# Router logits of the adaLN/FFN kernel: four column groups by tokens instead of by channels, turned by VectorE

## The reference, cut to what matters

```python
y = einsum('boi,bih->boh', agg_w, x) + agg_b[:, :, None]      # _L0_cond_ref, per sample
router_logits = y.reshape(-1, 1024) @ gate_w.T                # gate_w is 8 x 1024
routing = softmax(router_logits, axis=1)                      # 8 experts
in_scale, out_scale = routing @ in_channel_scale, routing @ out_channel_scale
out = y * in_scale @ sign(weight).T * out_scale + bias
x = x + out
```

## Time and profile before

| | us |
|---|---|
| median of 3 runs | 541.09 (540.41 to 542.42) |
| the profiled execution, own time | 541.51 |
| its span in the trace | 539.7 |
| TensorE busy (matmul records) | 523.5 |
| VectorE busy | 301.5 |
| ScalarE busy | 121.6 |
| GpSimd busy | 253.3 |

### The profile page before, as it was taken

One profiled execution on the slowest core, in us unless ns is written; L12 is line 12 of the kernel. 1 busy time (PEld: TensorE's weight loads), 2 busy tenths in 40 slices (PEclk: granted clock), 3 DMA queues, 4 the chain that ended last, 5 costly groups with the idle time before them and its releaser, 6 DMA issues.

```text
span 539.7 us, 14212 instructions
## 1 busy us (share of the span) xinstructions
PE 523.5 (97%) x5717; PEld 446.1 (83%) x5717; DVE 301.5 (56%) x482; ACT 121.6 (23%) x291; POOL 253.3 (47%) x121
## 2 busy tenths in 40 slices
PE   5897999999999999999999999999999999999997
PEld 4675778788787898898988988989889889898895
DVE  4579998797775654447446354364453634734411
ACT  5733334444434330101101011010010110101100
POOL 0028766766767398154263360651623616426100
PEclk9999999999999999999999999999999999999999
DMA  8696455554667362532413414224143162251111
GB/s 304 230 403 226 164 194 175 204 204 167 194 221 231 110 211 84 123 108 56 147 66 110 128 47 145 98 63 149 52 120 118 42 159 85 76 145 55 40 40 39
DMA packets 55049, 74.68 MB, mean 138 GB/s; under 512 B 6192, under 2 KB 41200, under 8 KB 55024
## 3 DMA queue, kind: packets, MB, share of 16 engines
q1 hardware_dynamic: 54800, 73.96, 42.4%
q10 hardware_dynamic: 224, 0.36, 0.3%
HBM read 57.50 MB, written 16.79 MB: 138 GB/s over the span
## 4 chain that ended last, share of the span: by engine, by line
PE 92%; DVE 4%; ACT 2%; issue 1%; DMA 1%; SPq 0%; DVEq 0%; ACTq 0%
PE bank L639 54%; PE bank L525 19%; PE bank L620 5%; PE bank L682 4%; PE bank L451 3%; PE bank L464 2%; PE bank L498 2%; DVE parts L978 1%; PE bank L601 1%; DVE y_t L949 1%; DMA cst<-in_consts 1%; ACT late L754 1%; PE bank L474 0%; PE bank L481 0%; DVE y_t L971 0%
## 5 line engine op out<-in xcount | busy, mean ns | idle before, releaser
L639 PE MATMUL bank<-early,parts 128*128 128x320 f32 (+1 forms) x1152 | 206.7, 337 | 0.0
L639 PEld LDWEIGHTS bank<-early,parts 128*128 128x128 f32 x1152 | 184.6, 188 | 16.6
L525 PE MATMUL bank<-late,parts 128*128 128x512 f32 x512 | 129.5, 403 | 2.1 <-DVE work L986 2.1
L525 PEld LDWEIGHTS bank<-late,parts 128*128 128x128 f32 x512 | 93.3, 190 | 23.0 <-DVE work L986 2.9
L1222 POOL TENSOR_TENSOR xs<-raw 128x1024 f32<-128x1024 f32 x14 | 26.5, 1894 | 157.1 <-DMA raw_turned<-x_scratch 157.1
L978 DVE TENSOR_TENSOR parts<-y_t,parts 128x512 fp32r<-128x512 f32 x64 | 95.0, 1503 | 2.5 <-ACT parts L785 1.0
L639 PE MATMUL bank<-late,parts 128*128 128x512 f32 x384 | 94.1, 394 | 0.0
L639 PEld LDWEIGHTS bank<-late,parts 128*128 128x128 f32 x384 | 70.9, 188 | 15.9
L1170 POOL TENSOR_TENSOR work<-work 128x512 f32<-128x512 f32 x32 | 46.3, 1448 | 47.3 <-DVE work L986 46.1
L1114 DVE TENSOR_TENSOR qk<-bank,qk 128x256 f32<-128x256 f32 x16 | 6.8, 424 | 102.1 <-ACT qk L874 102.1
L785 ACT ACTIVATE parts<-y_t 128x512 fp32r<-128x512 f32 x62 | 38.5, 631 | 88.3 <-DVE y_t L1093 46.1
(11 more groups left out here) (111 smaller groups left out, 484.7 us busy)
## 6 DMA issues: line engine op xcount, KB each, us to landing
xs<-in_x SPq DMA_DIRECT2D x16, 512.0 KB, 3.3
work<-in_x SPq DMA_DIRECT2D x16, 512.0 KB, 3.3
x_scratch<-work SPq DMA_DIRECT2D x16, 512.0 KB, 3.0
raw<-x_scratch SPq DMA_DIRECT2D x128, 64.0 KB, 2.9
work<-x_scratch SPq DMA_DIRECT2D x16, 512.0 KB, 3.6
out_tokens<-work SPq DMA_DIRECT2D x15, 512.0 KB, 2.7
raw_turned<-x_scratch SPq DMA_DIRECT2D x112, 64.0 KB, 2.5
stage<-in_wearly SPq DMA_DIRECT2D x8, 576.0 KB, 4.0
```

The lines of the kernel that those rows point to most:

```text
L525: last = mm(bank[4 + h][:, :], parts[:, p, a, c, :], signs[:, c, h * HALF:(h + 1) * HALF], start=(k % 16 == 0), stop=(k % 16 == 15))
L639: return mm(dst, parts[:, p, a, c, :], w(b, c), start=(k == 0), stop=(close and k == 23))
```

## The change

`product_logits` now gives column group t the tokens 32t to 32t+31 instead of a quarter of the channels. For each chunk c and each group t it multiplies the gate's 128x32 block with y_t's 128 channels x 32 tokens into partitions 32t to 32t+31, columns 0 to 31 of bank 2; all 8 chunks add up in each group. So 32 products with 32 moving columns take the place of 8 with 128, and each group holds a finished 32 (experts, padded) x 32 (tokens) block. VectorE transposes the four blocks in one instruction into SBUF (`turn_logits`), which gives 128 tokens x 32 with the 8 logits first. `copy_logits` on ScalarE and `sum_logits` on TensorE go, as do the selection matrix (8 columns of the constants) and their semaphores. `route_max` and `gate_exps` read SBUF. `product_scales` waits for `logits_turned` in place of `logits_copied`, `product_logits` for an earlier half of `scale_in` (two tiles back) in place of `gate_exp`, and `turn_logits` for `gate_exp` of the tile before.

```diff
             def product_logits(i, p, first_tile=False):
                 pe.wait_ge(y_biased, 4 * i + 2 * p + 2)
                 if not first_tile:
-                    pe.wait_ge(gate_exp, 2 * i + p)
+                    pe.wait_ge(u_ready, 4 * i + 2 * p - 3)
                 for c in range(L8):
-                    at = slice(EP * (c % 4), EP * (c % 4) + EP)
-                    made = mm(bank[2][at, 0:P], cst[:, C_GATE + c * EP:C_GATE + (c + 1) * EP], y_t[:, p, c, :],
-                              start=(c < 4), stop=(c >= 4))
+                    for t in range(P // EP):
+                        tokens = slice(EP * t, EP * t + EP)
+                        made = mm(bank[2][tokens, 0:EP], cst[:, C_GATE + c * EP:C_GATE + (c + 1) * EP], y_t[:, p, c, tokens],
+                                  start=(c == 0), stop=(c == L8 - 1))
                 made.then_inc(logits_made, 1)
-
-            def sum_logits(i, p, first_tile=False):
-                pe.wait_ge(logits_copied, 2 * i + p + 1)
-                if not first_tile:
-                    pe.wait_ge(u_ready, 4 * i + 2 * p - 1)
-                mm(bank[2][:, 0:E], logits_t[:, :], cst[:, C_SEL:C_SEL + E], start=True, stop=True).then_inc(logits_done, 1)
...
-            def product_scales(i, p, first_tile=False, copied=1):
+            def product_scales(i, p, first_tile=False, turned=1):
                 pe.wait_ge(routing_split, 2 * i + p + 1)
-                pe.wait_ge(logits_copied, 2 * i + p + copied)
+                pe.wait_ge(logits_turned, 2 * i + p + turned)
...
-                    if k == SUM_AT and two:
-                        sum_logits(*two)
...
-            def copy_logits(i, p):
-                act.wait_ge(logits_made, 2 * i + p + 1)
-                do(logits_t[:, :], bank[2][:, 0:P], ACT.Copy).then_inc(logits_copied, 1)
-
             def gate_exps(i, p):
                 act.wait_ge(gate_max, 2 * i + p + 1)
-                do(gate[:, 8:16], bank[2][:, 0:E], ACT.Exp, bias=gate[:, 0:1], accum_out=gate[:, 1:2]).then_inc(gate_exp, 1)
+                do(gate[:, 8:16], logits[:, 0:E], ACT.Exp, bias=gate[:, 0:1], accum_out=gate[:, 1:2]).then_inc(gate_exp, 1)
...
+            def turn_logits(i, p, first_tile=False):
+                dve.wait_ge(logits_made, 2 * i + p + 1)
+                if not first_tile:
+                    dve.wait_ge(gate_exp, 2 * i + p)
+                v.transpose(logits[:, :], bank[2][:, 0:EP]).then_inc(logits_turned, 1)
+
             def route_max(i, p):
-                dve.wait_ge(logits_done, 2 * i + p + 1)
-                v.tensor_reduce(gate[:, 0:1], bank[2][:, 0:E], AX.X, ALU.max, negate=True).then_inc(gate_max, 1)
+                dve.wait_ge(logits_turned, 2 * i + p + 1)
+                v.tensor_reduce(gate[:, 0:1], logits[:, 0:E], AX.X, ALU.max, negate=True).then_inc(gate_max, 1)
...
                 if four:
                     mix_kernels(*four)
+                if two:
+                    turn_logits(*two)
                 scale_out(i, p, 0)
                 scale_in(*one)
```

More of the change, by code:

```diff
@@ L52 @@
 C_W1, C_W2, C_CW = 162, 290, 298
-C_GATE, C_ID, C_SEL = 362, 618, 746
-C_RLO, C_SLO, C_SSG = 754, 755, 756
-C_END = 757
+C_GATE, C_ID = 362, 618
+C_RLO, C_SLO, C_SSG = 746, 747, 748
+C_END = 749
 PRODUCTS = ((0, 0), (0, 1), (1, 0))
-TURN_AT, BLOCK_AT, SUM_AT, CONV0_AT = 7, 18, 26, 4
+TURN_AT, BLOCK_AT, CONV0_AT = 7, 18, 4
 LORA_AT = 11
@@ L105, in adaln_ffn_kernel @@
         gate = sb("gate", [P, 64])
-        logits_t = sb("logits_t", [P, P])
+        logits = sb("logits", [P, EP])
         qk = sb("qk", [P, 2, NQK // 2])
@@ L173, in adaln_ffn_kernel @@
         logits_made = sem("logits_made")
-        logits_copied = sem("logits_copied")
-        logits_done = sem("logits_done")
+        logits_turned = sem("logits_turned")
         gate_max = sem("gate_max")
@@ L534, in _ @@
             product_logits(0, 0, True)
-            sum_logits(0, 0, True)
             inputs_of_y(0, 1)
@@ L554, in period0 @@
                             product_y(*three)
-                        product_scales(*one, copied=2 if two else 1)
-                    if k == SUM_AT and two:
-                        sum_logits(*two)
+                        product_scales(*one, turned=2 if two else 1)
                     ffn0_step(i, p, k)
@@ L563, in _ @@
                     pe.wait_ge(u_ready, 1)
-                    product_logits(0, 1)
+                    product_logits(0, 1, True)
                 if k == 10:
                     inputs_of_y(1, 0)
-                    sum_logits(0, 1)
                     product_y(1, 0)
@@ L574, in _ @@
                     product_y(1, 1)
-                    product_scales(0, 1, copied=2)
-                if k == 28:
-                    sum_logits(1, 0)
+                    product_scales(0, 1, turned=2)
                 ffn0_step(0, 0, k, True)
@@ L805, in round_u @@
                 round_parts(i, p, y_t[:, p], u_ready, u_hi, by_block)
-            copy_logits(0, 0)
             gate_exps(0, 0)
@@ L822, in _ @@
             copy_out_scale(0, 0, 1, False)
-            copy_logits(0, 1)
             gate_exps(0, 1)
@@ L827, in _ @@
             round_routing(0, 1)
-            copy_logits(1, 0)
             round_u(0, 1, True)
@@ L841, in period0 @@
                     round_stage(0, NW, (chunk + 1) * 16, early[:, 0, bass.ds(chunk, 1), :].rearrange("p a n -> p (a n)"))
-                if two:
-                    copy_logits(*two)
                 if one:
@@ L997, in _ @@
                                    ALU.mult, ALU.add).then_inc(scale_ready, 1)
+            turn_logits(0, 0, True)
             route_max(0, 0)
@@ L1010, in _ @@
             mix_kernels(1, 0)
+            turn_logits(0, 1)
             route_max(0, 1)
@@ L1015, in _ @@
             split_routing(0, 1)
+            turn_logits(1, 0)
             scale_out(0, 0, 0)
@@ L1262, in lay_out @@
     consts[:, C_GATE:C_ID].reshape(P, L8, EP)[:, :, 0:E] = turned(f["L0_ffn_gate_w"])
-    consts[:, C_SEL:C_SEL + E] = np.arange(P)[:, None] % EP == np.arange(E)[None]
     consts[:, C_ID:C_ID + P] = np.eye(P, dtype=np.float32)
```

## The result

The changed kernel takes 546.66 us in the median of 4 runs (546.31 to 547.10), the kernel before 541.75 beside it: ratio **1.0094**, 95% interval 1.0072 to 1.0116. It is slower by 5 us (0.9%); 540.0 was forecast, and 546.7 lies above the range. The price came from neither of the places where the prediction looked for one.

A forecast was written before the change was run, and what follows sets the result against it. TensorE, busy 97% of the span, was taken to bound the kernel. Sum -2.2 us and logits +1.1 us gave -1.1 us: 541.51 to 540.4, and 540.0 us with the median 0.4 us lower; range 538.8 to 544.4 us.

The forecast's parts named there:

- The sum goes: TensorE, dense stretch: dropping `sum_logits` from between the large products saves 0.22 us a tile, -2.2 us for ten tiles.
- The logits become 32 narrow products: TensorE's logits block, dense stretch: 0.68 us against 0.57, +0.11 us a tile, +1.1 us for ten.
- The straight line: Length of a logits round: 0.78 ns a column and 7 ns fixed, from 128 and 64 columns; 0.032 us at 32.
- Copy, transpose and the wait: ScalarE loses 16 copies, VectorE gains 16 transposes of 0.2 us; in the dense stretch nothing is lost.
- The start: Before 75 us: the third tile's logits still wait for a load of x until about 30.0 us; nothing gained.
- rival 1: Logits block: rounds do not shrink below 64 columns, block 1.10 us, kernel 544.2 us; 26 in 100.
- its own point of decision (0.79): From a logits block of 0.79 us on, a round of 0.039 us, the kernel is slower than before.
- Rivals 2 and 3: Logits records one after another, 551 us, 3 in 100; VectorE's transpose late, five periods wait, 542.0 us, 6 in 100.
- The 0.5 us at 43 us and its return: The scales' wait at 43.61 us shrinks by 0.5 us; TensorE's wait in the next block, near 56 us, gives it back.
- The range: Kernel time from 538.8 to 544.4 us, given 79 in 100.

The follow-up runs named there:

- experiment 5: The changed kernel with the logits of only the first 16 tokens of each group of 32, so 16 moving columns for 32; 546.19 us in one run.
- Experiments 1 and 2: Tiny unread products added: at 6 us to the changed kernel (544.27 to 541.63 us) and kernel before (541.91); ahead of kernel before's first four logits (546.12).

## Why the prediction was wrong

- **The sum goes, -0.22 us a tile: right.** 21 large products follow the scales in 99.12 - 94.19 = 4.93 us; in TensorE's timeline of before, the same 21 with the sum among them took 92.89 - 87.75 = 5.14. That is 0.21.
- **The logits become 32 narrow products, +0.11 us a tile: right in size, in part by luck,** 0.69 against 0.57, +0.12. The straight line was carried beyond its last point, and experiment 5 shows that it would have been wrong one step further: at 16 columns it gives 0.2 us less for the rounds, and 0.03 was measured. What sets a round at 32 columns is the floor of 0.033 us, and the line's 0.032 happens to lie on it. The rule of the Trainium skill ("TensorEngine Tiling (Array Packing)", Instruction Overhead: about 60 cycles a matmul) asked for y's 1.10 us here and is not what happens: 32 columns take 0.69. Its advice against tiling an already small dimension is right for the step to 16.
- **Copy, transpose and the wait: right.** 0.20 to 0.22 us for 0.2, no gap in the dense stretch. The period fell by 0.07 to 0.095 us where -0.11 was forecast; the ten tiles gave 0.9 us for 1.1.
- **The start: the step that failed.** "Late next is this load: nothing gained" and the words before it took the first 30 us as waits of the program alone and costed the edit's 96 more instructions a tile at nothing. The third tile's logits came 4.8 us late (34.8 us, forecast 30.0), the seventh's 6.4 us. Experiments 1 and 2 show that it is the number of instructions: with the block ends shifted, 2.4 to 5.0 us of the loss go (544.27 to 541.63); with the number given to the kernel before, the loss comes (546.12). The front got worse through a resource that the prediction touched once, in rival 1 ("the rate at which TensorE is fed has not been seen"), as a rate and only inside the dense block. The trace of before had the sign: the gap of 0.37 us ahead of 31.88 us inside y's products, with "issue" as its releaser, where no instruction waits. I had read it and left it out of the sum.
- **Rival 1** had the sign and half of the size, but not the mechanism: the block is 0.69 us, and by its own point of decision (0.79) the kernel should have been faster. Rivals 2 and 3 did not occur. The 0.5 us at 43 us and its return came as forecast, in a stretch that lies 5 us later: the wait ahead of the fourth tile's scales fell from 0.97 to 0.35 us, and one of 0.31 us stands ahead of the fifth tile's, on the transpose:

```profile
48.28 0.33 PE L490 MATMUL bank<-routing_t,scale_w 32*128 32x128 f32 x2 [0.35 <-issue]
...
62.01 0.33 PE L490 MATMUL bank<-routing_t,scale_w 32*128 32x128 f32 x2 [0.31 <-DVE logits L934]
```

- **The range** was made of known bounds for the products and none for the supply of instructions, so its upper end fell 2.3 us short.

The Trainium skill has the mechanism: "Runtime: NRT & Kernel Launch", section Instruction fetch mechanics, says that an engine's instructions come in blocks of 16 KiB, 256 of them, over a DMA queue of its own while the current block is executed, and that the crossing is mostly hidden. The 256 and the 0.02 MB packet agree with the trace. "Mostly hidden" held for the kernel before (0.37 us) and not for the changed one (3.95 and 1.77 us).

Why the dense stretch is free of it: the changed kernel's queues between 76 and 150 us hold only this row and none of instructions, so the loop's body is not received again.

```profile
q1 hardware_dynamic: 4704, 14.16, 57.8%
```

## What to carry to other kernels

Count instructions as well as time when a change replaces few products by many: in code that is run once, more instructions bring TensorE to the end of a block of 256 earlier, and where large loads fill the DMA engines it stood still there for up to 4 us, and then paid again at the lower clock. A gap with "issue" as its releaser inside a run of products that has no wait is the sign; a few idle instructions ahead of it that move it by exactly their number are the proof. In this kernel the same dense code inside the loop costs nothing of this.

## What the runs showed of the hardware

- A TensorE program block is 256 instructions (one 16 KB packet). 28 gaps in fourteen traces sat at counts 256 apart, each ended 1.2 to 1.5 us after such a packet, and one moved by 48 and 64 records for 96 and 128 added instructions.
- The packet of a block comes later behind data loads: with them it starts at 27.39 us and a gap of 3.95 us follows, with the loads held back it starts before 24.7 us and there is no gap.
- In four column groups, 64 float32 records with a weight load each take 0.69 us at 32 moving columns and 0.66 us at 16 (a round of four 0.034 and 0.033 us): below 32 columns next to nothing is gained.
- VectorE transposes 128x32 float32 out of PSUM in 0.20 to 0.22 us, between a 128x8 read (0.15) and a 128x128 copy (0.29).
